# Two layers of a graph network on one core: the fix-up's first quads reordered, a row operation put between the gate's two activations, and PSUM banks released singly

## What is computed

```python
# layer 1: attention over the edges of a destination, then a gate
alpha = segment_softmax(sum(q[dst] * (k[src] + ee)) / 4, dst)
out   = segment_sum((v[src] + ee) * alpha, dst)
x_r   = xm @ W_skip + b_skip                    # xm = x @ W_n2m
beta  = sigmoid(concat([out, x_r, out - x_r]) @ W_beta)
h     = layernorm(x + (beta * x_r + (1 - beta) * out) @ W_m2n)
# layer 2: dense product plus weighted messages
agg   = segment_sum((h @ w2)[src] * edge_weight, dst)
z     = layernorm(h + relu(h @ w1 + agg + b))
```

## Time and profile before

| | us |
|---|---|
| runs, median of three | 1712.65 |
| lowest and highest | 1708.18, 1715.38 |
| profiled execution | 1709.86 |
| its span, first to last instruction | 1708.3 |
| first loop, about | 30 to 655 |
| scans and carries, about | 655 to 715 |
| mixing stage, about | 715 to 1062 |
| second dense layer, about | 1062 to 1380 |
| fix-up, about | 1380 to 1708 |

### The profile page before, as it was taken

The page is one execution under the profiler, slowest core; times in us unless marked ns, Lnnn a source line. Parts: engine busy times, 40 slices in busy tenths (PEclk is TensorE's granted clock), DMA queues, the critical chain, the costliest instruction groups (busy, mean ns, idle before and its releaser), DMA issues.

```text
span 1708.3 us, 34719 instructions
## 1 busy us (share of the span) xinstructions
PE 1247.6 (73%) x9184; PEld 1102.6 (65%) x9184; DVE 1345.6 (79%) x5156; ACT 1224.4 (72%) x4231; POOL 1042.8 (61%) x1182
## 2 busy tenths in 40 slices
PE   1888888888888882278777876788878765576662
PEld 1777777777777772277666765666666665565651
DVE  2778888889988998878778876899999975465553
ACT  0899999999999994177787876899999952222220
POOL 2566666666656650055556555888888836676665
PEclk9999999999999996599999998999999988776785
DMA  6899999999999996734444445999999922222220
GB/s 195 268 304 306 309 301 306 305 304 305 299 299 300 304 306 232 226 126 149 146 149 156 151 142 183 287 288 292 284 287 289 293 98 84 73 90 80 75 88 32
DMA packets 210148, 372.00 MB, mean 218 GB/s; under 512 B 36740, under 2 KB 67821, under 8 KB 208935
## 3 DMA queue, kind: packets, MB, share of 16 engines
q1 hardware_dynamic: 120822, 200.48, 36.2%
q10 hardware_dynamic: 57771, 108.12, 17.3%
q0 software_dynamic: 31360, 61.17, 14.2%
HBM read 231.39 MB, written 161.37 MB: 230 GB/s over the span
## 4 chain that ended last, share of the span: by engine, by line
DVE 39%; ACT 20%; PE 15%; issue 11%; another core or an unknown queue 7%; POOL 4%; DMA 3%; SPq 1%; DVEq 1%; ACTq 0%; POOLq 0%
DVE hpre L1086 9%; DVE stats L980 9%; ACT scan_buf L724 5%; ACT hout L724 5%; ACT scan_buf L813 3%; PE pd L596 2%; DVE hpre L1226 2%; DVE val L1032 2%; POOL big L499 2%; PE pd L597 2%; DVE hpre L1296 2%; DVE ep L1070 2%; PE pd L565 2%; PE pk L619 1%
## 5 line engine op out<-in xcount | busy, mean ns | idle before, releaser
L980 DVE BATCH_NORM_STATS2 stats<-hpre 128x6 f32<-128x256 f32 x882 | 334.4, 420 | 1.8
L466 POOL DMA_INDIRECT ring_a<-in_x,gidx x196 | 186.1, 950 | 206.0 <-PE pt L556 137.0
L724 ACT ACTIVATE scan_buf<-hpre,nb,rs 128x128 f32<-128x128 f32 x686 | 291.8, 480 | 3.0 <-DVE scan_buf L990 0.9
L724 ACT ACTIVATE hout<-hpre,nb,rs 128x128 f32<-128x128 f32 x686 | 292.2, 480 | 1.5 <-DVE hout L990 0.8
L1086 DVE SCALAR_TENSOR_TENSOR hpre<-pd,beta,xg 128x128 f32<-128x128 f32 x784 | 221.2, 344 | 29.0 <-issue 0.5
L565 PE MATMUL pd<-w_sx,scan_buf 128*128 128x129 f32 x1568 | 230.1, 276 | 0.0
L469 POOL DMA_INDIRECT ring_b<-in_x,gidx x196 | 185.0, 944 | 60.3 <-issue 60.3
L619 PEld LDWEIGHTS pk<-w_sb,scan_buf 128*128 128x128 f32 x1568 | 211.1, 195 | 7.2
L499 POOL DMA_INDIRECT big<-h_tab,gidx x196 | 193.4, 987 | 34.8 <-POOL big L505 29.5
L619 PE MATMUL pk<-w_sb,scan_buf 128*128 128x128 f32 x1568 | 209.9, 277 | 0.0
L565 PEld LDWEIGHTS pd<-w_sx,scan_buf 128*128 128x128 f32 x1568 | 207.4, 192 | 2.7
(11 more groups left out here) (208 smaller groups left out, 3575.8 us busy)
## 6 DMA issues: line engine op xcount, KB each, us to landing
xg<-in_x SPq DMA_DIRECT2D x196, 256.0 KB
scan_buf<-in_xT SPq DMA_DIRECT2D x196, 256.0 KB
val<-h_tab SPq DMA_DIRECT2D x139, 256.0 KB
h_tab<-hout ACTq DMA_DIRECT2D x98, 256.0 KB
h_tab<-scan_buf ACTq DMA_DIRECT2D x98, 256.0 KB
out_z<-hout ACTq DMA_DIRECT2D x98, 256.0 KB
out_z<-scan_buf ACTq DMA_DIRECT2D x98, 256.0 KB
h_two<-h_tab SPq DMA_DIRECT2D x57, 256.0 KB, 8.5
```

The costliest lines, as they stand in the source:

```text
L466: gp.indirect_dma_start(out=ring_a[:, u, :], out_offset=None, in_=x[:, :], in_offset=bass.IndirectOffsetOnAxis(ap=gidx[:, k, 0:1], axis=0))\
L724: ins = act.activation(hout[ju][:, i * D:(i + 1) * D], hpre[:, ju, i * D:(i + 1) * D], ACT.Identity, bias=nb_of(ju, i), scale=rs_of(ju, i))
L980: ins = dve.bn_stats(stats[:, ju, i, :, :].rearrange("p j s -> p (j s)"), two)
```

## The change

Three edits in the first loop, one on the way into the fix-up.

1. Between its second and third row product DVE raises a new semaphore `half_d1`; PE waits for it ahead of the first bank, and for `pre_d1` only ahead of the second.
2. ACT issues the Relu of the gate, then one row operation of group k-3, then the Exp, then the other row operations. DVE computes the negated mean ahead of the four row products instead of behind them.
3. The mixing stage counts its Relus on `cl_d1` in place of a semaphore of its own.
4. The last running sums and the copies for the carry go ahead of the last two groups' row operations on DVE; the wait for ACT's last rows moves to quad 2. ACT evicts quads 0 and 1 ahead of the rows of groups 194 and 195. PE does the carry's transposes right after the product of quad 0 and the carry's product right after the transposes of quad 2, ahead of the product of quad 1.

```diff
@@ tensor, first loop
-                    if k > 1:
-                        pe.wait_ge(S["pre_d1"], k - 1)
                     for b in range(2):
+                        if k > 1:
+                            pe.wait_ge(S["half_d1"] if b == 0 else S["pre_d1"], k - 1)
@@ tensor, fix-up
-            def carry_products():
+            def carry_turns():
                 pe.wait_ge(S["sc"], 7)
...
+            def carry_product():
                 pe.wait_ge(S["sc"], 8)
...
             for k in range(T4 + 1):
-                if k == 3:
-                    carry_products()
...
+                if k == 2:
+                    carry_product()
                 if k > 0:
...
+                if k == 1:
+                    carry_turns()
@@ scalar, first loop
-                    exp_minus(act, em[:, u % 2, :], pd[:, u % 2, :, D], -1.0, S["cl_d1"], S["em_d1"], k)
+                    act.activation(em[:, u % 2, :], pd[:, u % 2, :, D], ACT.Relu, bias=top_c[:, 0:1], scale=-1.0)\
+                        .then_inc(S["cl_d1"], 1)
...
-                    scale_rows(gu, NJ - 1)
+                    scale_rows(gu, 1)
+                if live(k, 0, T):
+                    wait(act, S["cl_d1"], k + 1)
+                    act.activation(em[:, u % 2, :], em[:, u % 2, :], ACT.Exp, bias=top_c[:, 0:1], scale=-1.0)\
+                        .then_inc(S["em_d1"], 1)
+                if live(k, 3, T):
+                    scale_rows(gu, NJ - 1, 1)
@@ scalar, mixing stage
-                exp_minus(act, em[:, j % 2, 0:2], pd_bank[:, j % 2, :, D], 1.0, S["cl_b1"], S["em_b1"], j)
+                exp_minus(act, em[:, j % 2, 0:2], pd_bank[:, j % 2, :, D], 1.0, S["cl_d1"], T + j, S["em_b1"])
@@ scalar, end of the second dense layer
+            def c_evict(k):
+                u = k % 2
+                act.wait_ge(S["t_c"], k + 1)
+                if k > 1:
+                    act.wait_ge(S["mm_c"], k - 1)
+                else:
+                    act.wait_ge(S["mm_d2"], G - 1 + k)
+                act.activation(xgT[:, u, :], pd_bank[:, u, 0, :], ACT.Copy)
+                act.activation(xgT[:, 2 + u, :], pd_bank[:, u, 1, :], ACT.Copy).then_inc(S["tc_c"], 1)
+
             for g in range(G1, G + 5):
                 if g < G:
                     d2_evict(g)
+                if g - 2 >= G:
+                    if g - 2 < G + 2:
+                        c_evict(g - 2 - G)
@@ vector, first loop
+                if live(k, 2, T):
+                    g, gu, _ = back(k, u, it, 2)
+                    wait(dve, S["rs_d1"], g + 1)
+                    neg_mean(gu, NJ // 2).then_inc(S["nb_d1"], 1)
                 if live(k, 0, T):
...
+                        if i == 1:
+                            ins.then_inc(S["half_d1"], 1)
                     ins.then_inc(S["pre_d1"], 1)
-                if live(k, 2, T):
-                    g, gu, _ = back(k, u, it, 2)
-                    wait(dve, S["rs_d1"], g + 1)
-                    neg_mean(gu, NJ // 2).then_inc(S["nb_d1"], 1)
@@ vector, end of the second dense layer
+            def last_sums():
+                for t in range(done, T):
+                    run_sum(t)
+                dve.wait_ge(S["na_d2"], G - 2)
+                dve.wait_ge(S["run_b2"], T - 1)
+                dve.tensor_copy(sum_a, agg[:, T - 1, :])
+                dve.tensor_copy(sum_b, psame[:, T - 1:T].to_broadcast([P, D])).then_inc(S["sc"], 1)
+
             for g in range(G1, G + 3):
...
+                if g == G + 1:
+                    last_sums()
@@ vector, fix-up
+                    if k == 2:
+                        dve.wait_ge(S["na_d2"], G)
                     dve.wait_ge(S["mm_c"], k + 1)
```

More of the change, by code:

```diff
@@ L246, in gnn_kernel @@
             "piece_a", "log_a", "sc", "sc_pe", "sc_act",
-            "os_b1", "t_b1", "oT_b1", "mm_b1", "cl_b1", "em_b1", "xb_b1", "ep_b1", "be_b1", "pre_b1", "bn_b1",
+            "os_b1", "t_b1", "oT_b1", "mm_b1", "half_d1", "em_b1", "xb_b1", "ep_b1", "be_b1", "pre_b1", "bn_b1",
             "lv_b1", "rs_b1", "h_b1", "na_b1",
@@ L680, in inv_std, with exp_minus @@
             act.activation(r, log_v, ACT.Exp, scale=-0.5).then_inc(rs_sem, 1)
-        def exp_minus(act, e, logit, sign, cl_sem, em_sem, j):
+        def exp_minus(act, e, logit, sign, cl_sem, seen, em_sem):
             act.activation(e, logit, ACT.Relu, bias=top_c[:, 0:1], scale=sign).then_inc(cl_sem, 1)
-            wait(act, cl_sem, j + 1)
+            wait(act, cl_sem, seen + 1)
             act.activation(e, e, ACT.Exp, bias=top_c[:, 0:1], scale=-1.0).then_inc(em_sem, 1)
@@ L865, in _ @@
                             S["bn_c"], S["lv_c"], S["rs_c"], j)
[L866 to L872, removed]
+                if 2 <= k < T4:
+                    c_evict(k)
         @block.vector
@@ L1260, in _ @@
             done = 0
+            def last_sums():
[5 more added lines that the diff above has]
+                dve.tensor_copy(sum_b, psame[:, T - 1:T].to_broadcast([P, D])).then_inc(S["sc"], 1)
             for g in range(G1, G + 3):
-                ready = min(T, max(0, T * (g - G1) // (G - G1) - 6))
+                ready = max(0, T * (min(g, G) - G1) // (G - G1) - 6)
                 for t in range(done, ready):
@@ L1271, in _ @@
                     d2_stats(g - 1)
[L1272 to L1278, removed]
             dve.wait_ge(S["sc_pe"], 5)
```

## The result

The changed kernel takes 1707.6 us in the median of 20 runs (1698.4 to 1714.2), the kernel before 1714.3 in 20 runs beside them: ratio 0.9957, interval 0.9943 to 0.9972, so 5 to 10 us faster, 7.4 by the ratio. That is 0.43%, inside what was counted as the same, and 1.4 us above the forecast of 1706.2. The profiled execution has a span of 1699.84 us, 8.44 less than before.

| stretch | before, us | after, us | difference |
|---|---|---|---|
| start to the first gather | 29.57 | 27.52 | -2.05 |
| first gather to the last gather | 1343.88 | 1344.29 | +0.41 |
| last gather to the first scatter of the last stage | 28.05 | 20.37 | -7.68 |
| first scatter to the end | 306.78 | 307.66 | +0.88 |

A forecast was written before the change was run, and what follows sets the result against it. GpSimd's indirect DMAs, 1.555 us each, were taken to bound the kernel. Terms 0 + 0 + 0 - 6.4 us turned the profiled 1709.86 into 1703.5, or 1706.2 against the median of 1712.65; range 1703 to 1712.

The forecast's parts named there:

- counted as the same: Whole kernel: a measured difference within 0.5% (8.6 us) counts as no change; this outcome had chance 0.68.
- a pace of the indirect DMAs themselves: First loop and last stage: each indirect DMA takes GpSimd about 1.555 us, whatever waits, buffers and DMA load.
- while GpSimd works off its DMAs: First loop: TensorE's completions come through late during GpSimd's DMAs, making ScalarE's Relu wait 66 times, 20.6 us in all.
- Parts 1 to 3: First loop: banks released singly, row operation between Relu and Exp, negated mean earlier; each forecast to gain 0 us.
- VectorE's 2.91: First loop: VectorE's step without waits takes 2.91 us, the next limit once GpSimd's pace no longer hides ScalarE's saving.
- Rival A: First loop quickens from 3.11 to 2.91 us a step, 38 us, or 27 with only Relu waits gone; chance 0.15.
- Part 4: Start of the fix-up before the last stage: first fix-up and first scatter 6.4 us sooner, bounds 3 and 8.
- the product keeps its 3.82: Start of the fix-up: the product of quad 0 still takes 3.82 us, with TensorE at 1.2 GHz.
- the hidden copies: Start of the fix-up: carry copies are done by 1384.1, covered by the product of quad 0 ending at 1386.6.
- the 5.56 behind the fix-up: Before the last stage: from first fix-up to first scatter stays 5.56 us if three things stay covered.
- rival C: Start of the last stage: store, clock or scatter grouping cancels the gain, 0 to -3 us, 1711; chance 0.15.
- Rival B: First loop: Exp 0.27 us later after each late Relu, 18 us less 6.4, so 12 slower, 1724; chance 0.07.

The follow-up runs named there:

- set 2: Runs on one device in which the kernel before took 1578.5 us; the changed kernel measured again there had ratio 0.9873.
- half-rows kernel: Kernel before with each first-loop step's second gather fetching 64 rows instead of 128; ratio 0.9959 (kernel before 1578.5 us) and 0.9962 (1750.4 us).
- Warm: Changed kernel with twelve more bias products in TensorE's idle time before the product of quad 0; ratio 0.9859 to the kernel before at 1578.5 us.
- set 3: Runs on one device in which the kernel before took 1715.8 us and was profiled again; the first-loop edits without the fix-up edit had ratio 1.0007.
- set 1: Runs on one device, kernel before 1743.0 us; against it the fix-up edit alone had ratio 0.9984, the first-loop edits alone 1.0018.

## Why the prediction came out right

**The indirect DMAs set the loop's pace: right where it was read, wrong as a rule.** Leaving one of two out, or moving it to another queue at the same load, took 3.13 to 2.94 us a step. But the ground that the prediction gave, "a pace of the indirect DMAs themselves", failed in set 2: the last stage's scatters came 1.31 apart there, the loop's two gathers took 2.86 in the mean. What is GpSimd's own is 1.25 for a gather (0.944 and 0.30) and 1.28 for a scatter; the rest, up to 1.555, was there only in the sets in which TensorE has long idle times ended by "issue". The trace before held a sign of it: within a group of four the DMAs were 1.25 apart, and the rest of the 6.21 was one wait, ended by TensorE's transposes. Whether GpSimd or TensorE's lateness is the cause of the pace there, no run separates. That TensorE's side is late "while GpSimd works off its DMAs" fits the runs: the profile shows it as waits for "issue", and ahead of L562 they went when one gather did. Why it is so in some sets and not in another, on the same device number, stays open.

**Parts 1 to 3, nothing: right** at 1715 and 1743 us (1.0007 and 1.0018). ScalarE's 20 us turned into Relu waits, 23 us more of them. VectorE's 2.91 stayed in the stretch in which it was read the earlier trace rows; these are the first row products of two steps of the changed kernel:

```profile
645.46 1.13 DVE L1109 SCALAR_TENSOR_TENSOR hpre<-pd,beta,xg 128x128 f32<-128x128 f32 x4
...
648.37 1.13 DVE L1109 SCALAR_TENSOR_TENSOR hpre<-pd,beta,xg 128x128 f32<-128x128 f32 x4
```

But it is not the step of the whole loop: near 300 us a step of VectorE without a wait is 2.78. So where the indirect DMAs do not set the pace, parts 1 to 3 pay in the earlier part of the loop, and VectorE takes over behind it.

**Rival A fell here and holds elsewhere.** It had a chance of 0.15 and 27 to 44 us. At 1578 us the change gives 20 us, with a loop that quickens (worked out above from the half-rows kernel). The prediction weighed the Trainium skill (Perfetto Trace Analysis, DMA Instruction - SWDGE), which puts the recorded end at the last descriptor written. That GpSimd is free from there on was the prediction's own step; in the timelines the next DMA can start 0.30 behind the record of 0.94, in set 2 and within the groups of four alike. The group of four was indeed released by TensorE's transposes, as the rival had it, but earlier products and a shorter ScalarE step did not bring them sooner. The two-sided evidence of one trace could not tell the two conditions apart.

**Part 4, 6.4 us: right in mechanism, 1.3 short in this pair of profiles.** The term that was off is "the product keeps its 3.82", and with it the half clock for what follows it: 0.5 us in the product and 0.6 between the carry's transposes and its product. The eviction, the hidden copies and the 5.56 behind the fix-up were as forecast. Over all profiles the chain from the root to the first fix-up fell by 7.1 (14.2 to 7.1 in the mean), so part of the 1.3 is the pair. By the rule of the Trainium skill (TensorE: Matmul & The Clock Gate, What's actually happening), the half rate after idleness and the full rate after sustained work, the prediction gave 6.4 to 7.5. The trace agrees that the clock is back sooner, 0.83 where it was 0.50, but the 7.68 lies 0.2 above that range: that the product would begin at the full rate was not in it. "Warm" shows the term directly: a clock of 1.00 instead of a fall, and 1.4 us. The last store did not hold the scatter (rival C): it was issued at 1385.82, 6.0 behind the root where 8.2 was forecast, and more than 6 us ahead of the scatter.

**Rival B, the late gate, fell.** The Exp is later by 0.23 us at every step, and the loop grew by 1.0 us in the profile on record and by 0.8 in set 3, and was 0.9 shorter in set 1; none of this is 18.

## What to carry to other kernels

A pace that repeats to a hundredth in two stages of one trace can still be a condition of that execution and not a property of the instruction: look whether the queue's own pitch (record and gap, here 1.25) is shorter than the pace (1.555), and if so name what fills the rest before building on it. A wait that has grown names no bound either: compare the step with the work of each engine in several windows of the loop. A change that is worth nothing under one bound can be worth a per cent where that bound is away; time it where the kernel's time differs. To judge a few us in a hand-over, measure from the last common event to the first dependent one in several profiles: the start-up alone moved by 12 us between executions, the chain of one kind of kernel by at most 1.5.

## What was not expected of the hardware

- The kernel before took 1578.5, 1715.8, 1743.0 and 1750.4 us in four sets. The first loop, the mixing stage and the last stage differ (loop 574 us at the one end and 625 at the other for the changed kernel), the gathers ahead of the last stage do not (308 to 310).
- In the slower sets TensorE shows idle time ended by "issue", up to 6.5 us at once and 60 us in the last stage in set 3 (29.8 and 9.8, with 20 on its other lines); in set 2 none there.
- An indirect DMA of 64 rows costs GpSimd almost what one of 128 costs: records of 0.91 and 0.944 us.
- One small transfer ahead of the first loop was waited for 1.6 to 3.5 us in eleven profiles and 17 in three; the first gather started at 27 to 31.5 us in eleven profiles and at 39.2 to 39.7 in three.
